# One scatter in flight at a time: GpSimd waits for each landing before it issues the next

## The reference, cut to what matters

```
x = x + attention(layernorm_over_channels(x))      # kq shared, 32 wide; softmax over 256 pixels
t = tokens(x)                                      # (2048, 64)
logits = layernorm(t) @ router_w.T                 # 8 experts
gates  = top-2 of softmax(logits), normalised
y_e    = w2[e] @ (silu(w1[e] @ tn) * (w3[e] @ tn)) # hidden width 682
t = t + sum over the 2 chosen experts of gate * y_e
```

## Time and profile before

| | us |
|---|---|
| median of 3 runs without a profile | 175.12 (175.03 to 176.37) |
| span of the profiled execution, first to last instruction | 238.2 |
| PE busy in the profile | 166.9 (70%) |
| GpSimd busy in the profile | 85.7 (36%) |

### The profile page before, as it was taken

One profiled execution on the slowest core, in us unless ns is written; L12 is line 12 of the kernel. 1 busy time (PEld: TensorE's weight loads), 2 busy tenths in 40 slices (PEclk: granted clock), 3 DMA queues, 4 the chain that ended last, 5 costly groups with the idle time before them and its releaser, 6 DMA issues.

```text
span 238.2 us, 4880 instructions
## 1 busy us (share of the span) xinstructions
PE 166.9 (70%) x1682; PEld 139.1 (58%) x1682; DVE 99.7 (42%) x372; ACT 70.8 (30%) x141; POOL 85.7 (36%) x114
## 2 busy tenths in 40 slices
PE   3595957428683069589494994958949697895683
PEld 2364836307452068588393983948839597783543
DVE  2557568255583037584222433223232344342230
ACT  2377433013310034224232142222422323333101
POOL 2963577723277700603205033060230604142400
PEclk9999586555578559979799598895997979798579
DMA  6990000184570229652958075390661600000053
GB/s 185 322 297 20 11 25 22 31 267 151 159 290 23 50 81 328 216 210 46 364 169 313 3 240 196 88 346 4 203 228 42 266 10 14 11 15 11 17 176 91
DMA packets 19893, 33.00 MB, mean 139 GB/s; under 512 B 7691, under 2 KB 13100, under 8 KB 19868
## 3 DMA queue, kind: packets, MB, share of 16 engines
q1 hardware_dynamic: 16732, 29.55, 37.8%
q0 software_dynamic: 2272, 2.35, 3.0%
q10 hardware_dynamic: 864, 0.79, 1.0%
HBM read 25.55 MB, written 7.13 MB: 137 GB/s over the span
## 4 chain that ended last, share of the span: by engine, by line
issue 48%; POOL 21%; PE 11%; DVE 8%; DMA 3%; another core or an unknown queue 3%; ACT 3%; POOLq 1%; SPq 0%; ACTq 0%; DVEq 0%
POOL ys L370 15%; POOL xs L361 5%; PE psum L925 3%; PE psum L914 2%; ACT xn L426 2%; DMA y_in<-ys 2%; DVE rows L595 1%; PE psum L894 1%; PE psum L1103 1%; PE psum L885 1%; DMA ys<-y_out,y_row 1%; DMA proj<-projections 1%; DVE index L606 1%; DVE neg_max L584 1%
## 5 line engine op out<-in xcount | busy, mean ns | idle before, releaser
L370 POOL DMA_INDIRECT ys<-y_out,y_row x39 | 37.4, 960 | 104.0 <-DVE y_out L839 95.2
L827 DVE TENSOR_TENSOR hid<-psum,act_sb 128x512 f32<-128x512 f32 (+1 forms) x50 | 33.4, 676 | 88.9 <-ACT act_sb L504 61.6
L1031 PE MATMUL psum<-x_cols,weights 64*128 64x128 f32 x390 | 52.9, 286 | 13.9 <-issue 12.1
L1031 PEld LDWEIGHTS psum<-x_cols,weights 64*128 64x128 f32 x390 | 47.6, 193 | 19.4 <-issue 15.8
L1033 PE MATMUL psum<-x_cols,weights 64*128 64x128 f32 x390 | 53.1, 286 | 0.9 <-issue 0.9
L504 ACT ACTIVATE act_sb<-psum 128x512 f32<-128x512 f32 (+1 forms) x50 | 28.7, 586 | 70.0 <-remote 42.4
L1033 PEld LDWEIGHTS psum<-x_cols,weights 64*128 64x128 f32 x390 | 47.7, 193 | 1.1 <-issue 1.1
L1059 PE MATMUL psum<-hid,weights 128*64 128x128 f32 x468 | 42.8, 357 | 2.1 <-issue 1.1
L1059 PEld LDWEIGHTS psum<-hid,weights 128*64 128x64 f32 x468 | 39.3, 189 | 4.8 <-issue 2.7
L361 POOL DMA_INDIRECT xs<-xrows,pos x32 | 31.6, 987 | 12.9 <-issue 8.9
L1037 PE MATMUL psum<-x_cols,weights 64*106 64x128 f32 x78 | 8.7, 349 | 23.1 <-ACT act_sb L504 18.4
(11 more groups left out here) (148 smaller groups left out, 189.9 us busy)
## 6 DMA issues: line engine op xcount, KB each, us to landing
weights<-experts SPq DMA_DIRECT2D x39, 565.0 KB
xs<-zeros SPq DMA_DIRECT2D x4, 1040.0 KB, 11.1
x_in<-xs SPq DMA_DIRECT2D x39, 32.5 KB
ys<-y_out,y_row POOLq DMA_INDIRECT x39
xs<-xrows,pos POOLq DMA_INDIRECT x32
y_in<-ys ACTq DMA_DIRECT2D x2, 256.0 KB, 4.5
y_in<-ys SPq DMA_DIRECT2D x2, 256.0 KB, 4.3
x_sb<-x_tok SPq DMA_DIRECT2D x1, 384.0 KB, 3.4
```

The lines of the kernel that those rows point to most:

```text
L370: nc.gpsimd.indirect_dma_start(ys, bass.IndirectOffsetOnAxis(ap=y_row[:, j:j + 1], axis=0), y_out[:, i % RING, h, :], None).then_inc(y_sca ...
L827: nc.vector.tensor_tensor(live(i, hid[:, i % 2, s, :]), live(i, H3_BANK[g % 3]), live(i, act_sb[:, g % 3, :]), ALU.mult).then_inc(hid_done, 1)
L1031: first_ = nc.tensor.matmul(H1_BANK[g % 2][:, src], weights[0:C, slot, P * s:P * (s + 1)], x_cols[0:C, i % 2, src], start=True, stop=True)
```

## The change

Each scatter now waits until the one before it has landed. A row scatter waits for all row scatters before it. A result scatter waits for those of its own quad before it; the first of a quad has no new wait, and the last quad (`i + 1 < NQ` is false) has none at all. In numbers: 31 of the 32 row scatters and 27 of the 39 result scatters get a wait. Nothing else is changed.

```
+            def landed_before(p, at):
+                k = phase_of(p)
+                n = 16 * (TPP * K_TOP * (p - (KNOWN[k - 1] if k else 0)) + at)
+                if n:
+                    pool.wait_ge(dispatched[k], n)
+                elif k:
+                    pool.wait_ge(dispatched[k - 1], 16 * TPP * K_TOP * (KNOWN[k - 1] - (KNOWN[k - 2] if k >= 2 else 0)))
+
             def scatter_row(p, at):
+                landed_before(p, at)
                 if at % K_TOP == 0:
                     pool.wait_ge(tn_ready, TPP * p + at // K_TOP + 1)
...
                 if h == 0:
                     pool.wait_ge(y_out_ready, i + 1)
                     pool.wait_ge(y_row_ready, i + 1)
+                elif i + 1 < NQ:
+                    pool.wait_ge(y_scattered[i % RING], 16 * (sum(len(members(k)) for k in range(i % RING, i, RING)) + h))
                 nc.gpsimd.indirect_dma_start(
```

## The result

The changed kernel takes 252.8 us (252.2 to 254.2) against 175.8 for the one before: 1.444 times as long, with a 95% interval of 1.436 to 1.452. I had forecast 226, with a range of 197 to 240. The direction and the place were right, the size was 27 us short.

The account below looks back on a forecast made before the run. The prediction took GpSimd's serial scatters as the bound: rows to 102.6, nine quads of results to 178.8, last landing 183.5, 12.2 us of end to 195.7, plus 30 contention: 226 us, range 197 to 240.

Parts of the forecast that it names:

- The plain run rebuilt from the profile: Unchanged kernel without the profile's stalls: first `y_out` ready at 78.4, then 9.1 us a quad, paced by PE.
- GpSimd as the bound, both stages in one chain: GpSimd runs 32 row scatters, then 39 result scatters, in one program order that sets the end; 195.7 us without contention.
- U: GpSimd's time from one waiting scatter's start to the next, outside weight loads: 2.40 us, 1.13 more than now.
- I take 30: Contention: 30 us added to GpSimd's chain for scatters that land late inside the ten loads of weights.
- upper end of 41: Upper bound of contention: 1.8 scatters lost a load at 2.40 us, 4.2 us a load, 41 us in ten loads.
- C: Start-to-start time of a waiting scatter inside a load of weights: 2.40 + 3.0 = 5.4 us.
- The deviations: GpSimd's four `t_deviation` computations in the row stage: run while a landing is awaited, costing about 0.3 us together.
- What lies around the span: Time of a run outside its span, at the kernel's ends: the prediction added nothing for it.
- Rival A: Waits on GpSimd's scatters cost only their plain landing, as queues take turns; contention near zero, 196 us, chance 0.10.
- Rival B: Result waits hide behind the quads and only row scatters cost: 184 us, chance 0.04.
- Rivals C and D: C: spread scatters disturb weight loads less, 163 us, chance 0.02; D: landing always precedes next issue, 175 us, chance 0.01.

Follow-up runs that it names:

- experiment with late waits: The kernel before, with the change's waits on the result scatters of quads 7 and 8 alone, none on row scatters: ratio 1.008 (1.002 to 1.014).

## Why the prediction was right about the place and wrong about the size

**The plain run rebuilt from the profile.** Right within 3 us. I had the first `y_out` ready at 78.4 and 9.1 us a quad. The experiment with late waits has the first ready at 76.04 + 0.42 = 76.5 and the last at 156.7, which is 9.2 us for each of 8.75 quads, and the copies of quads 3 to 5 at 105.2, 114.2 and 123.2, 9.0 us apart. Timed runs of the kernel before have spans of 172.5 to 175.8, so the 63 us were the profile's. PE does set the pace of the quads, but the figure that I gave in support, 9.8 us of PE work at the full clock, was too long for a step of 9.1: in a run with late result waits one quad is 8.97 us of PE work at a granted clock of 1.00.

**GpSimd as the bound, both stages in one chain.** Right: the result stage starts 50 us later with the row waits than without and takes about as long, and GpSimd's waits head the table.

**U = 2.40 us.** Right: 2.44 to 2.46 in the row stage, 2.40 in the result stage. Over 31 row steps that is up to 1.6 us more.

**"I take 30" for contention.** This is the step that failed. From the waits of the changed kernel: 69.8 - 27 x 1.44 = 30.9 us in the result stage and 60.1 - 28 x 1.50 = 18.1 in the row stage, 49 us, 19 more than taken and 8 more than my upper end of 41. The price of one delayed scatter was right: C was 5.4 us from start to start, and the 15 steps beside a load have a mean of 5.4. As C came from a single scatter, and they run from 2.9 to 7.7, that is partly luck. What was wrong is how many pay it. 30 us are ten scatters at 3.0 us, one a load. My upper end had 14, as many as fit one after the other into 75 us of loading, and I took 11 us off for scatters near a load's end and for the free step of each quad. The runs show no such relief: 15 scatters were delayed in 78 us of loading, 44 us in all. A scatter near a load's end pays less, but that is already in the mean of 5.4, and behind the free step the next scatter waits all the same. The other 4 to 5 us are the three landings beside a packet of the instruction queue, for which the prediction had no term.

**The deviations "which run while a landing is awaited and cost about 0.3 together".** Wrong. I asked what GpSimd queues behind its waits, and not who waits for that. VectorE waits for the deviation of pair 2, and GpSimd later for VectorE: 1.1 us before the 17th row scatter and 3.7 before the 19th, 4.8 in all; taking it out gave 3 to 4 us back. The trace of the kernel before had the sign of it, GpSimd standing for VectorE's moments ahead of such a deviation:

```profile
51.85 0.23 POOL L348 TENSOR_SCALAR variance_t<-moments_t 128x4 f32<-128x4 f32 x1 [3.87 <-DVE moments_t L627]
```

**What lies around the span.** I took nothing; the run is 1.7 to 3.2 us longer than its span.

The sum made again: 226 + 19 (contention) + 1.6 (U) + 0.7 (first scatter at 26.3) + 4.8 (deviations) - 0.3 - 1.1 (no wait between the last row and the first result scatter) = 250.7, against a span of 251.3. It is made from the same profile, so that it closes shows only that no large term is missing.

**Rival A and the rule behind it.** The chance of 0.10 was too high. By the Trainium skill, "DMA: Bandwidth & Descriptors", section "Queues, rings and completion order", the engines take turns between queues packet by packet. I read that as one row of a load and took the delay as near 0. The same sentence of the Trainium skill says that such a packet is typically some 9 to 17 descriptors. An estimate from that page's figure, if a descriptor is one row of 4520 bytes and 348 GB/s (1.46 MB in 4.2 us) are shared by 16 engines: 1.9 to 3.5 us for one turn of the load. In the trace the first packet of a scatter comes 4.1 to 4.2 us after its start in the two rows shown, against 1.5 to 1.7 in the open, so 2.5 us later. So the rule as stated isn't against the measurement; my reading of it was too short. No run here shows how many rows an engine takes in one turn. The other argument for A, and for C, was a misreading too: the loads that I took as free of GpSimd's packets or less disturbed, 336 and 344 GB/s, have them as the slower ones do. Queue 0 in 153.0 to 160.6 (336 GB/s), 168.9 to 176.1 (344) and 97.5 to 105.8 (294), all of the kernel before:

```profile
q0 software_dynamic: 116, 0.12, 4.5%
q0 software_dynamic: 77, 0.08, 3.1%
q0 software_dynamic: 96, 0.10, 3.5%
```

**Rival B.** In the open it is true: two quads of waits cost some 0.3 to 3 us. With loads running it isn't, 31 to 34 us.

**Rivals C and D.** Excluded, as expected: the plain landing is 2.13 us, and `dispatched[0]` was complete at 71.3.

## What to carry to other kernels

A DMA whose landing is awaited before the next is issued costs its whole latency each time. Beside large loads on another queue that latency was 2.4 times the plain one in the mean here, and each waiting scatter paid it anew. So count all that can fit into the loading time, and take nothing off without a row that shows the relief. A second one in flight took 70 of 77 us off. To price a new wait, list both what is queued behind the waiting instruction on its engine and who waits for each item of that list.

## What the runs showed of the hardware

- A scatter of 33 KB lands in 2.13 us from its start when nothing else runs. The 15 that were awaited beside a 2.3 MB load of weights made steps of 2.9 to 7.7 us, 5.4 in the mean, where the plain step is 2.4; in the two rows shown the first packet came 4.1 to 4.2 us after the start. With the weights in packets of half the size the longest wait of the result stage was 4.8 us rather than 6.1.
- Three awaited scatters with no load beside them took 1.3 to 1.6 us more than plain, each with one 16 KB packet of the instruction queue in its window.
- The same bytes loaded in rows of 2260 bytes rather than 4520, with twice the DMAs, made the kernel before 10% slower: SyncE issued one such DMA every 0.5 us, and its round of a quad grew by 2 us and more, to 11.2 in the rows shown.
- The profile of the kernel before is 63 us longer than its timed runs. All ten experiments and the changed kernel have spans within 3 us of their runs. What stopped PE, VectorE and ScalarE in that one profile stays open.
